# Two attentions: evictions placed between a round's exponentials, low parts placed behind the round's maxima

## The reference, cut to what matters

```python
x = x + L0_xattn(layernorm(x), ctx)     # "A": 16 heads of 64, 508 text keys + 4 image keys
x = x + L0_ffn(layernorm(x))            # "M": mixture of 8 experts, top 2
x = x + L1_xattn(layernorm(x), ctx)     # "C": 8 heads of 64, 512 keys
x = x + L1_ffn(layernorm(x))            # "F": gate/up/down with quantised values
# each attention, for 4 batches of 512 queries:
q = x @ Wq; k = ctx @ Wk; v = ctx @ Wv
s = einsum('bhid,bhjd->bhij', q, k) * 64 ** -0.5
p = softmax(s); o = einsum('bhij,bhjd->bhid', p, v)
y = merge_heads(o) @ Wo + bias          # A adds low-rank terms and a second softmax over the image keys
```

## Time and profile before

| | |
|---|---|
| median of 3 runs | 1096.37 us (1090.71 to 1099.45) |
| the profiled execution | 1091.27 us, its span 1089.5 us |
| PE busy | 903.8 us (83%) |
| DVE busy | 779.3 us (72%) |
| ACT busy | 726.2 us (67%) |
| POOL busy | 622.3 us (57%) |
| loop of A, first to last scores | 54.4 to 495.5 us |
| loop of C, first to last scores | 756.7 to 962.9 us |

### The profile page before, as it was taken

How to read it: one execution, slowest core, us unless ns; L and a number is a source line. 1 busy time by engine, 2 the same in 40 slices (tenths; PEclk the granted TensorE clock), 3 DMA queues, 4 the chain that set the end, 5 groups by cost and what they waited for, 6 DMA issues and landing times. The chain is left out here.

```text
span 1089.5 us, 23585 instructions
## 1 busy us (share of the span) xinstructions
PE 903.8 (83%) x8849; PEld 689.9 (63%) x8854; DVE 779.3 (72%) x1550; ACT 726.2 (67%) x1222; POOL 622.3 (57%) x571
## 2 busy tenths in 40 slices
PE   4887999999999999997546999968888989973486
PEld 4655686767776777675435999956566767663143
DVE  5768778778877887676785444438888786747796
ACT  3387978788878888884442444435697878952674
POOL 2177766766686667673425555442686867853142
PEclk9899999999999999998867999989799999986698
DMA  9579999899989998996741222253999989983155
GB/s 262 172 129 186 162 151 157 143 187 149 172 149 172 158 156 137 158 172 100 240 150 56 76 74 78 69 191 114 175 167 201 155 157 150 182 136 116 27 118 126
DMA packets 455248, 158.80 MB, mean 146 GB/s; under 512 B 428097, under 2 KB 445697, under 8 KB 455105
## 3 DMA queue, kind: packets, MB, share of 16 engines
q1 hardware_dynamic: 451392, 147.06, 70.5%
q0 software_dynamic: 3744, 10.23, 3.0%
HBM read 38.62 MB, written 12.71 MB: 47 GB/s over the span
## 5 line engine op out<-in xcount | busy, mean ns | idle before, releaser
L477 POOL TENSOR_TENSOR A_PHL<-A_pr,A_PHL 128x508 f16<-128x508 f32 x256 | 294.9, 1159 | 133.5 <-ACT A_pr L754 132.6
L753 ACT ACTIVATE A_PHL<-A_ps,A_negmax 128x508 f16<-128x508 f32 x256 | 179.2, 700 | 17.5 <-DVE A_negmax L1003 14.8
L477 POOL TENSOR_TENSOR C_PHL<-C_pr,C_PHL 128x512 f16<-128x512 f32 x128 | 150.2, 1183 | 55.9 <-ACT C_pr L754 55.3
L754 ACT ACTIVATE A_pr<-A_ps,A_negmax 128x508 f32<-128x508 f32 x256 | 181.1, 707 | 0.0
L1003 DVE TENSOR_REDUCE A_negmax<-A_ps 128x2 f32<-128x1016 f32 x128 | 154.2, 1205 | 0.0
L598 PE MATMUL A_ps<-A_K,A_Q 64*128 64x512 f32 x768 | 123.7, 427 | 12.4 <-ACT A_pr L754 9.7
L616 PE MATMUL A_ps<-A_VH,A_PT 128*128 128x65 bf16 (+1 forms) x1024 | 109.5, 197 | 18.7 <-DMA A_PT<-A_PHL 18.4
L616 PEld LDWEIGHTS A_ps<-A_VH,A_PT 128*128 128x128 f16 (+1 forms) x1024 | 93.6, 98 | 47.3 <-DMA A_PT<-A_PHL 29.8
L617 PE MATMUL A_ps<-A_VL,A_PT 128*128 128x64 f16 (+1 forms) x1024 | 108.5, 194 | 0.0
L618 PE MATMUL A_ps<-A_VH,A_PT 128*128 128x65 bf16 (+1 forms) x1024 | 108.3, 195 | 0.0
L753 ACT ACTIVATE C_PHL<-C_ps,C_negmax 128x512 f16<-128x512 f32 x128 | 88.7, 693 | 15.9 <-DVE C_negmax L1003 15.2
(11 more groups left out here) (349 smaller groups left out, 2653.2 us busy)
## 6 DMA issues: line engine op xcount, KB each, us to landing
A_PT<-A_PHL SPq DMA_TRANSPOSE x256, 3.4
M_WINl<-in_L_ffn_w_in SPq DMA_DIRECT2D x4, 1024.0 KB, 11.8
M_WOUTl<-in_L_ffn_w_out SPq DMA_DIRECT2D x4, 1024.0 KB, 12.6
C_yc<-routed_rows SPq DMA_DIRECT2D x8, 512.0 KB, 5.5
ct_split<-A_CT SPq DMA_DIRECT2D x4, 768.0 KB, 4.2
C_CT<-ct_split SPq DMA_DIRECT2D x4, 768.0 KB, 7.8
M_rows<-M_xn SPq DMA_DIRECT2D x4, 512.0 KB, 9.0
out<-X SPq DMA_DIRECT2D x16, 128.0 KB, 2.0
```

Source lines behind the costliest of these rows:

```text
L477: pool.tensor_tensor(PHL[:, e % PRING, 1, 0:KEYS], pr[:, e % RING, 0:KEYS], PHL[:, e % PRING, 0, 0:KEYS], ALU.subtract).then_inc(pl_ready. ...
L753: a.activation(PHL[:, e % PRING, 0, 0:KEYS], o, ACT.Exp, bias=nm[:, n % 4, h:h + 1])
L754: a.activation(pr[:, e % RING, 0:KEYS], o, ACT.Exp, bias=nm[:, n % 4, h:h + 1]).then_inc(p_ready.sem, 1)
```

## The change: what it does

On ACT, pass g still makes the exponentials of round g-1, but the projections it evicts are now those of step g-1 instead of those of step g, and it does so between the exponentials of the first head and those of the second. On DVE, `low` of the projections of step g-1 stays in pass g, but moves behind the maxima of round g. PE, POOL and SP keep their order, and no instruction is added or removed.

```diff
-            def weights(n):
+            def weights(n, between):
...
                     a.activation(pr[:, e % RING, 0:KEYS], o, ACT.Exp, bias=nm[:, n % 4, h:h + 1]).then_inc(p_ready.sem, 1)
+                    if h == 0:
+                        for u in between:
+                            high(u)
...
-            for g in range(G + TAIL):
-                if 1 <= g <= G:
-                    weights(g - 1)
-                for u in at.get(g, []):
-                    if u[0] in HI_KINDS:
+            for g in range(1, G + TAIL + 1):
+                rows = [u for u in at.get(g - 1, []) if u[0] in HI_KINDS]
+                if g <= G:
+                    weights(g - 1, rows)
+                else:
+                    for u in rows:
                         high(u)
...
             for g in range(G + TAIL + 1):
-                for u in at.get(g - 1, []):
-                    low(u)
                 if g < G:
                     wait(v, s_filled, g + 1)
...
                     v.tensor_reduce(nm[:, g % 4, :], ps[:, S_BANK + 2 * (g % 2):S_BANK + 2 * (g % 2) + 2, 0:KEYS], AX.X,
                                     ALU.max, negate=True).then_inc(max_ready.sem, 1)
+                for u in at.get(g - 1, []):
+                    low(u)
+                if g < G:
                     nb = g // U + 1
```

## The result

The changed kernel takes **1291.57 us** (median of 4 runs, 1290.31 to 1294.63), against 1096.28 us for the kernel before (4 runs). The ratio is 1.179, with a 95% interval of 1.173 to 1.184. The forecast was 1245, with a range that ended at 1285: the sign and the new waits were right, the size fell short by 47 us, and the measured time lies 7 us beyond the range.

A forecast was written before the change was run, and what follows sets the result against it. PE was taken to set the pace of both loops. The profiled 1091.3 us, plus new waits of 103 (A) and 32.5 (C), less 9 of old waits, plus 27 for half clock, gave 1245 us; range 1190 to 1285.

The forecast's parts named there:

- The bound: A's and C's loops: PE sets the pace, busy 414.6 of 445.6 us and 183.6 of 209.3.
- The wait at a due projection: PE, bank used two projections before, in the preceding step: start 2.96 us behind scores instead of 0.89, 2.07 us lost.
- Behind a y: PE projections whose late bank held a y: shorter add on DVE, 0.41 instead of 0.68 us, so wait 1.80 us.
- The count and the sum of waits: PE in both loops: 59 such steps in A, 13 in C; new waits 103 us in A, 32.5 in C.
- credits: Old PE waits that go: about 6 us for exponentials and 2 for transfers in A, 1 in C; 9 us.
- the scores that wait for K: Short rounds where K's low part now follows the maxima: 10 us in A, 3.4 plus 3.6 in C.
- The move on ACT: First two exponentials go ahead of evictions; sum of work unchanged, helping at most 9.7 us in A; evictions no further limit.
- The clock: Half-clock stretches after PE's new waits in both loops, 1.4 us each; about 38 waits of 2 us or more, 27 us taken.
- the second, the clock falling behind nearly every long wait: Rival for both loops: all 38 long waits cost 1.4 us, 1270 us, with late transfers up to 1285; chance 0.2.
- The shallower waits: Rival for both loops: stretched rounds let ACT, POOL and transfers catch up, absorbing today's PE idle time; 1167 us, chance 0.12.
- the faster case: Rival: first two exponentials no longer wait for an eviction, regaining all 22 us of PE's waits; 1069 us, chance 0.04.

The follow-up runs named there:

- the change where it isn't due: Against the kernel before, evictions and low parts moved only for projections PE's next step does not need; 1088.41 us, ratio 0.994.
- due low parts first: Changed kernel, but low parts that PE's next step needs made ahead of the maxima again; 1133.30 us, ratio 1.035 to the kernel before.

## Why the prediction was right in its waits and wrong in its clock

**The bound** (PE sets the pace of both loops): right. PE had next to no idle time that could take up the new waits: some 147 us of them came, 25 us of old ones went, and the idle time of the loops rose by 121.5.

**The wait at a due projection**: right to the hundredth. 2.96 us was forecast for step 58, 2.97 measured; 2.07 us for the wait, 2.08 at step 57. Behind a y, 1.80 was forecast, and the six waits of the o transposes for y (line 887) are 11.0 us together, 1.83 each.

**The count and the sum of waits**: right for the due projections, and partly by luck in the total. Waits of 135.5 us less credits of 9 made 126.5 us; PE's idle time in the loops rose by 121.5. A: 94.6 forecast net, 94.4 measured; C: 31.5 and 27.1. The waits of the due projections, 118 us of this, measured 117. But the scores that wait for K were put at 17 us and took 27, and the credits at 9 us and came to 25: the waits for exponentials and transfers fell by 6.4 and 9.0 us in A, and by 8.7 and 0.5 in C. The two misses are of opposite sign, and the sum hides them.

**The move on ACT**: half right. I said that the later evictions are no limit so long as the low parts come behind the maxima; the run with the DVE part alone has 6 us less idle time in A, so this is nearly so. What I didn't weigh is that the ACT part costs 68 us alone. The forecast treated it as neutral, and it is only hidden by the larger wait.

**The clock**: this is the step that failed. "I take half the waits, 27 us", with 53 as the upper end. Measured: 79 us of longer busy time, and 183 us more at half clock (142 + 71 less 9 + 21). The price of a microsecond at half clock was sound: the two rounds of C give 1.4 us for 3.2 us at half clock (twice 0.32 of 5.01), which is 0.44, and 79 for 183 is 0.43. The number of stretches was not, nor their length. The trace has 43 more of them (49 less 6), while I allowed 19 and at most 38, and one cost 1.8 us on the mean instead of 1.4, as some last longer than the one that I priced, up to 13.7 us.

Why too few: I counted only the waits of 2 us or more, and halved them against my own rows, which said two of three. I left out the waits of 1.8 us and those of the scores for K; with all of them PE has 66 idle times over 1.5 us, and half clock began in 46 of them or right behind. Those of steps 56, 57, 58 and 60 are examples, that of 59 is an exception. In the kernel before it was 6 of 10, so the share is much the same there, and the runs do not show that it matters whether waits follow each other step by step. Two of three of the waits down to 1.7 us that I had listed, 51, at 1.4 us would have made 48 us: nearer, and still 31 short. With the measured 79 us in place of the 27 my sum is 1297, near the 1291.8 of the profiled execution, so no other step is needed to explain the miss. The Trainium skill that I cited, "TensorE: Matmul & The Clock Gate", section "A second HAM failure mode: psum-queue depth-cycling", says that the clock swings between its two levels where PE idles briefly between groups of matmuls while it cycles through PSUM banks. The trace agrees, with 49 stretches at half clock, and the case should have been given more than 0.2.

**The rivals.** The one that came nearest is the second, the clock falling behind nearly every long wait, and the time went past its own 1270 to 1285; the late transfers that were to make up the last 15 us did not come, as PE's waits for transfers shrank. The shallower waits are excluded by the idle time, and the faster case by the ratio. What stands behind the faster case, exponentials that need not wait for an eviction, is real, as the run with the change where it isn't due shows, but there it took 4.6 us off the waits and 7 off the kernel, not 22.

**What stays open**: why the DVE part alone has less half clock in A (103 us) than both parts (142) at nearly the same idle time. Over both loops it has 63 idle times over 1.5 us and 43 stretches at half clock, against 66 and 49. The two differ in when the evictions end and so in how the work lies around the waits; no run separates this.

## What to carry to other kernels

When two engines hand a few buffers back and forth, write down for every step which release the next step needs, and keep those ahead of anything that waits for work the other engine has only just begun; only the others are free to move. When a change makes the matmul engine wait again and again for 2 us, price its work at half clock too, and count every wait for it, not only the longest: here the waits cost 121 us and the clock another 79, and 955 useless matmuls put into the waits took 56 us off again.

## What the runs showed of the hardware

- Idle times of PE of about 2 us can bring it to half clock: in the loops of the changed kernel 46 of 66 over 1.5 us had half clock begin in or right behind them, in those of the kernel before 6 of 10. In steps 57 and 58 the clock alternates between 1.00 while PE waits and 0.50 while it works.
- Much idle time in short pieces brought little of it: with the ACT part alone PE idles 69 us in A's loop, 40 more than before, at a clock of 0.97; with the whole change it idles 123 us at 0.88.
- The clock can be held by work without use: with it PE is idle 39 us in A's loop at a clock of 0.98, and with half of it 77 us at 0.97, in the same time (1235.4 and 1234.2 us).
- The part ahead of A's loop, which no experiment touches, ended between 53.1 us (the changed kernel) and 61.3 us (due low parts first) in the profiled executions. Differences of a few us between kernels are therefore better read from the loops than from the span.
